# Indirect transfers at most two in flight, expert rows loaded two ahead, and full products in the last groups of an attention and expert kernel

## What is computed

```python
xn = layernorm(x)                                  # x: 8 batches x 512 rows x 128
x + attention(xn) + experts(xn)
# attention: 16 heads of 8 columns; softmax(q k^T / sqrt(8), masked) v, then wo
# experts: 8 experts, each row goes to its 2 best by the gate's logits, at most 1280 rows
#   per expert; gelu(rows @ c_fc[e] + fc_bias[e]) @ c_proj[e] + proj_bias[e],
#   weighted by the two router probabilities and added
```

## Time and profile before

| | us |
|---|---|
| median of 3 runs (lowest, highest) | 716.48 (712.72, 718.2) |
| the profiled execution | 716.14 |
| its span, first to last instruction | 714.3 |
| busy: PE, DVE, ACT, POOL | 618.3, 406.7, 394.9, 229.0 |
| mean granted clock of TensorE, of full | 0.88 |

### The profile page before, as it was taken

How to read it: one execution, slowest core, us unless ns; L and a number is a source line. 1 busy time by engine, 2 the same in 40 slices (tenths; PEclk the granted TensorE clock), 3 DMA queues, 4 the chain that set the end, 5 groups by cost and what they waited for, 6 DMA issues and landing times.

```text
span 714.3 us, 9757 instructions
## 1 busy us (share of the span) xinstructions
PE 618.3 (87%) x3526; PEld 322.6 (45%) x3526; DVE 406.7 (57%) x601; ACT 394.9 (55%) x775; POOL 229.0 (32%) x230
## 2 busy tenths in 40 slices
PE   4767999599999999989778867969999999899884
PEld 2433443223333343358767766869334333224312
DVE  5758598458888979831111110111798988857602
ACT  3442067357778877883144134323877787655751
POOL 3856911623343431200110011010255566322310
PEclk9989599759999999999789989889999999756955
DMA  6887044211212121422133033211312122111120
GB/s 191 248 277 233 21 180 155 72 38 51 73 54 74 59 68 39 119 67 74 34 107 104 27 84 108 64 45 38 102 47 76 48 73 80 58 43 27 47 66 15
DMA packets 57999, 60.44 MB, mean 85 GB/s; under 512 B 8032, under 2 KB 42848, under 8 KB 57952
## 3 DMA queue, kind: packets, MB, share of 16 engines
q1 hardware_dynamic: 52160, 45.92, 21.3%
q0 software_dynamic: 5792, 13.90, 6.3%
HBM read 29.65 MB, written 29.62 MB: 83 GB/s over the span
## 4 chain that ended last, share of the span: by engine, by line
PE 52%; DVE 21%; DMA 8%; ACT 6%; SPq 5%; issue 4%; POOL 1%; another core or an unknown queue 1%; DVEq 0%; POOLq 0%; ACTq 0%
DVE nmax L765 14%; PE bPV L983 14%; PE bX L967 12%; PE bD L1074 12%; DMA xe<-slot_x 5%; PE bD L948 5%; ACT probs L621 4%; PE bPV L1109 2%; PE bX L957 2%; DMA k_rows<-hid 2%; PE bD L991 1%; PE bD L1002 1%; DVE ye L808 1%; SPq L368 1%; DVE attn L783 1%
## 5 line engine op out<-in xcount | busy, mean ns | idle before, releaser
L765 DVE TENSOR_REDUCE nmax<-bD 128x2 f32<-128x1024 f32 x256 | 300.5, 1218 | 76.5 <-PE bD L948 58.7
L621 ACT ACTIVATE probs<-bX 128x512 f32<-128x512 f32 x512 | 268.2, 597 | 114.7 <-PE bX L967 102.6
L967 PE MATMUL bX<-Q,K 27*128 27x512 f32 x512 | 186.4, 503 | 19.0 <-ACT probs L621 12.6
L983 PE MATMUL bPV<-probs,v_aug 128*32 128x512 f32 x1024 | 152.0, 668 | 1.6 <-ACT probs L621 0.7
L967 PEld LDWEIGHTS bX<-Q,K 27*128 27x128 f32 x512 | 76.0, 196 | 163.5 <-ACT probs L621 111.3
L948 PE MATMUL bD<-K,Q 25*128 25x512 f32 x512 | 137.2, 508 | 10.7 <-DVE nmax L765 7.4
L1074 PE MATMUL bD<-wpj,hid 128*128 128x128 f32 x640 | 88.2, 306 | 11.4 <-DVE xeT_lo L798 6.3
L1074 PEld LDWEIGHTS bD<-wpj,hid 128*128 128x128 f32 x640 | 85.8, 220 | 14.8 <-issue 14.8
L512 POOL DMA_INDIRECT slot_x<-xn_all,put_i x64 | 62.4, 975 | 90.3 <-PE bPV L983 76.4
L649 ACT ACTIVATE hid<-bX,fcb 128x512 f32<-128x512 f32 (+1 forms) x96 | 55.5, 615 | 47.1 <-PE bX L1063 46.5
L948 PEld LDWEIGHTS bD<-K,Q 25*128 25x128 f32 x512 | 58.6, 197 | 47.1 <-DVE nmax L765 29.8
(11 more groups left out here) (104 smaller groups left out, 488.3 us busy)
## 6 DMA issues: line engine op xcount, KB each, us to landing
K<-k_rows SPq DMA_DIRECT2D x128, 50.0 KB
Q<-q_rows SPq DMA_DIRECT2D x128, 48.0 KB
slot_x<-hid POOLq DMA_DIRECT2D x10, 512.0 KB, 3.0
xe<-slot_x SPq DMA_DIRECT2D x8, 640.0 KB, 6.3
slot_y<-ye SPq DMA_DIRECT2D x8, 640.0 KB, 4.3
q_rows<-hid SPq DMA_DIRECT2D x8, 512.0 KB, 3.7
k_rows<-hid SPq DMA_DIRECT2D x8, 512.0 KB, 5.4
acc<-in_x SPq DMA_DIRECT2D x8, 256.0 KB, 4.9
```

Of the source, the lines that this page charges most:

```text
L621: taken(nc.scalar.activation(probs[:, (g % 2) * 4 + i, :], next_x()[:], ACT.Exp, scale=SCALE))
L765: nc.vector.tensor_reduce(nmax[q][:, k, 2 * pair:2 * pair + 2], bank()[:], AX.X, ALU.max, negate=True).then_inc(s_dd, 1)
L967: filled(nc.tensor.matmul(next_x()[:], K[u][rows_used, q, j * P:(j + 1) * P], Q[u][rows_used, q, :], start=True, stop=True))
L983: last = nc.tensor.matmul(bPV[32 * h:32 * h + 32, :], v_aug[b % 2][:, j, u * UH + QUAD * q + h, :], probs[:, (g % 2) * 4 + h, :], start=(g ...
```

## The change

- POOL: the zero fill keeps two DMAs in flight on two semaphores. Puts and gets also use two semaphores each, and each waits for the last but one of its kind; they no longer wait for groups. The addition of `bo` to `acc`, one instruction of 4096 columns ahead of the zero fill, becomes eight of 512 columns after every second of the first 16 puts.
- SP: the rows of expert e + 2 are asked for when those of e + 1 have been turned, ahead of the wait for the results of e.
- `LEAD` is 7 instead of 8, and `COMBINED_AT` is 109, 116 and 123.
- PE: in groups of the last turn with nothing ahead, two products of 512 columns over all rows take the place of `ahead`. Ahead of the third head index of the lead, `keep_clock` runs eight products instead of three.

```diff
-LEAD = 8
+LEAD = 7
...
-COMBINED_AT = {GROUPS_BEFORE + 9 + 7 * b: b for b in range(COMBINED_BY_POOL, B - 1)}
+COMBINED_AT = {GROUPS_BEFORE + 13 + 7 * b: b for b in range(COMBINED_BY_POOL, B - 1)}
...
             def experts():
-                sp.wait_ge(s_put, KN * 16)
+                for q in range(2):
+                    sp.wait_ge(s_put[q], KN // 2 * 16)
                 load_rows(0)
+                sp.wait_ge(s_dd, rows_item(0, NCH - 1) + 1)
+                load_rows(1)
                 for e in range(E):
-                    if e < E - 1:
-                        sp.wait_ge(s_dd, rows_item(e, NCH - 1) + 1)
-                        load_rows(e + 1)
+                    if e + 2 < E:
+                        sp.wait_ge(s_dd, rows_item(e + 1, NCH - 1) + 1)
+                        load_rows(e + 2)
...
-            pool.wait_ge(s_xn, B)
-            nc.gpsimd.tensor_tensor(acc[:], acc[:], bo_s[:, None, :].to_broadcast([P, NT, C]), ALU.add).then_inc(s_bo, 1)
             pool.wait_ge(s_fill, 7)
             for h in range(ZERO_DMAS):
                 pool.dma_start(slot_x.rearrange("(p h r) c -> h p (r c)", p=P, h=ZERO_DMAS)[h], hid_f[:, 0:per]
-                               ).then_inc(s_zero, 16)
-                pool.wait_ge(s_zero, h * 16 + 16)
+                               ).then_inc(s_zero[h % 2], 16)
+                wait(pool, s_zero[1 - h % 2], (h + 1) // 2 * 16)
+            pool.wait_ge(s_xn, B)
+            pool.wait_ge(s_zero[(ZERO_DMAS - 1) % 2], ZERO_DMAS // 2 * 16)
             for k in range(TOPK):
                 for n in range(NT):
                     col = k * NT + n
-                    pool.wait_ge(s_pv, put_after(col))
+                    wait(pool, s_put[col % 2], col // 2 * 16)
                     pool.indirect_dma_start(slot_x, bass.IndirectOffsetOnAxis(ap=put_i[:, col:col + 1], axis=0),
                                             xn_all[:, n, :], None, bounds_check=SLOTS - 1, oob_is_err=False
-                                            ).then_inc(s_put, 16)
+                                            ).then_inc(s_put[col % 2], 16)
+                    if col < 2 * B and col % 2 == 1:
+                        b = col // 2
+                        nc.gpsimd.tensor_tensor(rows(acc, b), rows(acc, b), bo_s[:, None, :].to_broadcast([P, TT, C]),
+                                                ALU.add).then_inc(s_bo, 1)
...
                         col = k * NT + b * TT + n
-                        pool.wait_ge(s_pv, got_after((b * TOPK + k) * TT + n))
+                        if k * TT + n >= 2:
+                            pool.wait_ge(s_get[b][n % 2], (k * TT + n) // 2 * 16)
+                        elif b > 0:
+                            pool.wait_ge(s_get[b - 1][n % 2], TOPK * TT // 2 * 16)
...
                     elif not last:
                         scores_for_max(b + 1, 0, head - GB, pair)
+                    else:
+                        nc.tensor.matmul(free()[:, 1, :], ones_r[:], hot_f, start=True, stop=True)
...
-                        keep_clock(3)
+                        keep_clock(8 if (s, pair) == (2, 0) else 3)
```

More of the change, by code:

```diff
@@ L72 @@
 GROUPS_BEFORE = (EXPERTS_AFTER + 1) * GB + 4
-def put_after(i):
-    return 4 + i * (GROUPS_BEFORE - 16) // KN
-def got_after(i):
-    return GROUPS_BEFORE + 1 + i * (B * GB - GROUPS_BEFORE - 4) // KN
-COMBINED_AT = {GROUPS_BEFORE + 9 + 7 * b: b for b in range(COMBINED_BY_POOL, B - 1)}
+COMBINED_AT = {GROUPS_BEFORE + 13 + 7 * b: b for b in range(COMBINED_BY_POOL, B - 1)}
 class Count:
@@ L247, in build @@
         s_slots = sem("s_slots")
-        s_put = sem("s_put")
+        s_put = [sem("s_put0"), sem("s_put1")]
         s_chain = sem("s_chain")
@@ L263, in build @@
         s_split = sem("s_split")
-        s_zero = sem("s_zero")
+        s_zero = [sem("s_zero0"), sem("s_zero1")]
         s_slot = sem("s_slot")
-        s_get = [sem(f"s_get{b}") for b in range(B)]
+        s_get = [[sem(f"s_get{b}{q}") for q in range(2)] for b in range(B)]
         s_comb_p = sem("s_comb_p")
@@ L525, in combine @@
             def combine(b):
-                pool.wait_ge(s_get[b], TOPK * TT * 16)
+                for q in range(2):
+                    pool.wait_ge(s_get[b][q], TOPK * TT // 2 * 16)
                 got = xn_all[:, b * TOPK * TT:(b + 1) * TOPK * TT, :].rearrange("p (k n) c -> p k n c", k=TOPK)
@@ L540, in _ @@
                         col = k * NT + b * TT + n
-                        pool.wait_ge(s_pv, got_after((b * TOPK + k) * TT + n))
+                        if k * TT + n >= 2:
+                            pool.wait_ge(s_get[b][n % 2], (k * TT + n) // 2 * 16)
+                        elif b > 0:
+                            pool.wait_ge(s_get[b - 1][n % 2], TOPK * TT // 2 * 16)
                         pool.indirect_dma_start(gathered(b, k * TT + n), None, slot_y,
                                                 bass.IndirectOffsetOnAxis(ap=get_i[:, col:col + 1], axis=0),
-                                                bounds_check=SLOTS - 1, oob_is_err=False).then_inc(s_get[b], 16)
+                                                bounds_check=SLOTS - 1, oob_is_err=False).then_inc(s_get[b][n % 2], 16)
                         if 0 < b <= COMBINED_BY_POOL and (k, n) == (0, 2):
@@ L787, in take_out @@
             def take_out(b):
-                dve.wait_ge(s_bo, 1)
+                dve.wait_ge(s_bo, b + 1)
                 take()
@@ L823, in combine @@
             def combine(b):
-                dve.wait_ge(s_get[b], TOPK * TT * 16)
+                for q in range(2):
+                    dve.wait_ge(s_get[b][q], TOPK * TT // 2 * 16)
                 dve.wait_ge(s_dd, d.value())
@@ L913, in _ @@
             d = Count()
+            hot_f = hot[:].rearrange("p n e -> p (n e)")
             def free():
@@ L1101, in _ @@
             pe.wait_ge(s_hot, 1)
-            hot_f = hot[:].rearrange("p n e -> p (n e)")
             nc.tensor.matmul(bX[1][:], prefix_r[:], hot_f, start=True, stop=True)
```

## The result

The changed kernel takes 753.94 us (median of 4 runs, 750.12 to 763.25) against 717.34 us: ratio 1.0515, 95% interval 1.0431 to 1.0599. The prediction said 659 us. The profiled execution took 750.12 us, span 748.3, which is 34.0 us over the span of before. Runs of one kernel differ by up to 7% here, as the clock falls at other groups from run to run, and the ratios with an interval compare each kernel's least disturbed runs; where there are too few of these, only medians are given.

A forecast was written before the change was run, and what follows sets the result against it. The prediction took PE as close to its bound in full-clock attention, with losses from waits and the half clock they leave. From 716.14 us, -35.5 + 18.6 - 9.7 - 15.4 - 6 - 9 = -57.0 gave 659 us, range 638 to 698.

The forecast's parts named there:

- Experts, -35.5: Experts: rows asked for two ahead end PE's wait and half clock, periods 25.51 to 19.59 us, gaining 35.5 us.
- `LEAD` 7, +18.6: Attention, every fourth group: maxima come late, PE waits 0.6 us at 31 places, losing 18.6 us (6 to 25).
- the rival that the new gap drops the clock: Attention: the gap ahead of the maxima halves the clock in most groups, 1.3 us for some 75; about 757 us, 3%.
- Lead, -9.7: Lead: fewer pairs and a clock kept full bring group 0 from 93.09 to 83.4 us, gaining 9.7 (11.3 to 6.3).
- the second condition: Lead: DMAs of the first maxima may hold group 0 until at most 86.8 us; 83.4 was taken.
- Indirect transfers, -15.4: Attention under the puts: earlier puts, two in flight, end a stall, gaining 15.4 us (bounds 15.4 gained, 74 lost).
- the one stall that the term was read from: Attention during thirteen puts, 124.41 to 140.37: ScalarE and VectorE fell idle, half clock until 158.20; 15.4 us lost.
- backlog: Puts in attention: piled-up requests were supposed to cause the stall, so the cap of two would end it, gaining 15.4 us.
- rate rival: Attention under transfers: each of 128 slows others 0.3 us, 697 us, 12%; or the run itself stalls, 733 us, 7%.
- the 7% rival: Attention under the puts: the run of 64 itself stalls ScalarE and VectorE; 733 us, over 800 with the gets; 7%.
- VectorE's combines, -6: Groups 109 and 116 onward: moved combines cause less waiting and half clock, gaining 6 us (0 to 11).
- Full products at the end, -9: Last groups: full products hold the clock there and behind them, at no counted cost, gaining 9 us (0 to 10).

The follow-up runs named there:

- its own profile: The kernel before with only the change's part on transfers: 712.84 us against 719.16, no interval.
- the late run with the limit: Kernel before with the transfer part, additions of `bo` ahead of the puts, first put waiting for group 11, two puts in flight: 703.05 us, ratio 1.0066.
- the pair of late runs: Kernel before with the transfer part, additions ahead, first put waiting for group 11: 796.71 us without limit, 703.05 us with two puts in flight.
- the fifth of them: Kernel before with the transfer part, no put limit, additions of `bo` ahead, first put waiting for group 11: 796.71 us against 716.03.

## Why the prediction was wrong

1. *Experts, -35.5:* right, -36.5, by the mechanism and the period given.
2. *`LEAD` 7, +18.6: the step that failed.* The wait was sized well: full groups at the maxima take 3.74 to 3.94 us for 3.16 to 3.30, the 0.6 us foreseen, and with half clock in the way it came to 12.4 us in all. What failed is the sentence "At half clock the wait would be hidden, but little half clock should be left", which put the clock behind the wait at nothing, and with it the 3% for the rival that the new gap drops the clock. Its ground was that 1.40 us had done it and that the gap is below 1 us. The trace shows the clock falling at a wait of 0.51 us, after 24.2 us in which PE stood 1.5 us longer than at the same place with `LEAD` 8. It does not fall at each such wait, and three of the falls lie at waits that a GpSimd instruction drew out to 0.98 to 2.48 us, which the term did not have either. `LEAD` 7 alone on the kernel before cost 46.7 us of half clock for 13.8 of waits; in the changed kernel half clock cost 59.5 us more than before, 42.8 of it in the turns between lead and end. The rival's 757 us were right to 3 us, partly by chance: it had the other gains whole.
3. *Lead, -9.7:* the full products held the clock from 66 to 87, and the second condition that the prediction named, the DMAs of the maxima, then bound (1.90 us at 86.64). Group 0 came 4.2 us earlier, and groups 0 to 8 then took 14.9 us more than before, at half clock. With `LEAD` 8 group 0 came 8.3 us earlier (88.6), and those groups were at half clock all the same. The term ended at group 0 and left out what the clock does behind it.
4. *Indirect transfers, -15.4:* the size is right to a tenth in its own profile, whose groups 0 to 66 lose the one stall that the term was read from; in time no run shows it (0.99 by the medians, and 1.0066 for the late run with the limit). The reason is half right: a limit ends the stall where it came (the pair of late runs), but there was no backlog in that stall, and here the earlier beginning and the additions between the puts would have ended it without a limit. Neither rate rival came in the changed kernel, and in four kernels without a limit puts at 1.28 us left the groups under them as they were. That a run by itself can stall, the 7% rival, the fifth of them shows: 797 us. The term also left out the freed gets, which cost some 4 us at groups 95 to 97 in its own profile.
5. *VectorE's combines, -6:* not gained. Group 109 still takes 4.72 us, and in the next group the clock falls; group 116 lies at half clock anyway. That it is they, and that they were worth far more than 6, the kernel with them on GpSimd shows (33 us between the two profiles from group 109 to the end, ratio 0.91 for 0.95).
6. *Full products at the end, -9:* with the clock at full they hold it, and are worth 3.4 us against the kernel before (25.6 for 29.0) and 1.8 behind group 126 (12.9 for 14.6 us to the end), 5 in all; with the clock at half they cost 10.6 (44.4 for 33.8). "I count no cost" is wrong in both states: 0.5 us a group at full clock, 1.4 at half.

Terms 2, 3, 5 and 6 went wrong together: each took it for granted that the clock is at full where it starts. The sum added them as if they were independent, but they hang on one thing, so that a bad case is not one term's but all of theirs.

## What to carry to other kernels

Where a core's clock falls with its load, price a new wait on the critical engine by the groups that may then run at half speed, not by its own length: `LEAD` 7 alone cost 13.8 us of waits and 46.7 of clock. That a longer gap once dropped the clock does not make a shorter one safe. Put work into an unavoidable gap, or move the waiting instruction to where its input has long been there. Products that are to hold a clock have to come while it is still up; in the last groups at half clock they cost 10.6 us and did not bring it back in the changed kernel. And look which GpSimd instruction runs beside a short VectorE instruction that the critical engine waits for.

## What the runs showed of the hardware

- The granted clock fell at a wait of 0.51 us, after PE had been busy 21.86 of 24.20 us, and held at one of 1.00 us after 21.79 of 24.20; once down, it stayed at half through a stretch in which PE was busy 56.47 of 59.00 us. A busy PE does not by itself bring it back; in the attention it mostly came back in groups 0, 1 or 8 of a turn.
- A run of 64 indirect writes from GpSimd, 1.28 us apart, went with ScalarE and VectorE idle for most of 80 us (busy 7.68 and 8.25 us), while its own transfers were moved within 3.0 us each; in four other kernels 64 such writes without a limit, in two of them without any pause, did nothing of the kind, with PE busy 96% of 59 us in one. For much of the idle time the profile has no releaser ("remote"). With two in flight instead of no limit it did not come.
- VectorE's `CAST` and `TENSOR_TENSOR` of 16 columns took 0.18 us, and up to 1.3 us where they began beside one `TENSOR_TENSOR` of GpSimd, ending with it (64 of 74); up to 2.8 us where it was several GpSimd instructions in a row.
- An indirect put of 64 KB took 2.3 us (median; 2.27 to 4.19) from its issue to its landing, in the one trace that has it.
